# Conversions and tanh of the Scalar engine placed behind the second exponential of an even step

## What is computed

```python
q, k, v = (split_heads(x @ W.T + b) for W, b in ...)      # 16 heads of 16
scores = jnp.einsum('hbnd,hbmd->hbnm', k, q) * SCALE      # 1024 x 1024 per head, SCALE = 1/16
attn = jax.nn.softmax(scores, axis=-1)
x = layernorm(x + einsum('hbnm,hbmd->hbnd', attn, v) merged @ Wo.T + bo)
gate, up = x @ wg.T, x @ wu.T                             # hidden 768, weights int32 / 127
x = layernorm(x + (silu(gate) * up) @ wd.T)
```

## Time and profile before

| | |
|---|---|
| median of 3 runs | 2783.86 us |
| the profiled execution | 2781.8 us, its span 2779.7 us |
| TensorE busy | 2633.4 us, 95% of the span |
| Scalar engine busy | 2132.9 us, 77% |
| VectorE busy | 1291.1 us, 46% |
| GpSimd busy | 543.2 us, 20% |
| granted TensorE clock, mean | 0.994 |
| batch 0 / each batch 1 to 14 / steps of batch 15 | 149.4 / 168.1 to 168.5 / 147 us |

### The profile page before, as it was taken

One profiled execution on the slowest core, in us unless ns is written; L12 is line 12 of the kernel. 1 busy time (PEld: TensorE's weight loads), 2 busy tenths in 40 slices (PEclk: granted clock), 3 DMA queues, 4 the chain that ended last, 5 costly groups with the idle time before them and its releaser, 6 DMA issues. The chain is left out here.

```text
span 2779.7 us, 47000 instructions
## 1 busy us (share of the span) xinstructions
PE 2633.4 (95%) x17294; PEld 943.7 (34%) x17294; DVE 1291.1 (46%) x2812; ACT 2132.9 (77%) x2370; POOL 543.2 (20%) x542
## 2 busy tenths in 40 slices
PE   6889999999999999999999999999999999999996
PEld 2223332333324333342333323333243333424233
DVE  3324445454444544445444454544445444454536
ACT  2877777777787777777877787777777777787881
POOL 2101122121222112121121221112121121221113
PEclk9999999999999999999999999999999999999998
DMA  4111021210202102121120202102021020211101
GB/s 150 47 45 61 24 82 31 58 59 20 92 21 77 47 21 85 32 74 39 35 79 24 85 29 74 50 13 92 27 79 39 21 92 24 78 36 54 26 9 38
DMA packets 81742, 144.08 MB, mean 52 GB/s; under 512 B 27584, under 2 KB 29504, under 8 KB 79424
## 3 DMA queue, kind: packets, MB, share of 16 engines
q1 hardware_dynamic: 79968, 139.81, 16.4%
q10 hardware_dynamic: 1504, 0.66, 0.1%
HBM read 88.48 MB, written 50.33 MB: 50 GB/s over the span
## 5 line engine op out<-in xcount | busy, mean ns | idle before, releaser
L567 ACT ACTIVATE probs<-psum 128x1024 f32<-128x1024 f32 x2048 | 1991.3, 1026 | 548.0 <-PE psum L978 547.2
L978 PE MATMUL psum<-probs,v 128*32 128x512 f32 x8192 | 987.5, 600 | 0.8 <-ACT probs L567 0.8
L978 PE MATMUL psum<-kstack,qstack 51*128 51x512 f16 x4096 | 673.5, 383 | 87.2 <-ACT probs L567 74.8
L978 PEld LDWEIGHTS psum<-kstack,qstack 51*128 51x128 f16 x4096 | 144.9, 93 | 825.9 <-ACT probs L567 483.5
L978 PEld LDWEIGHTS psum<-probs,v 128*32 128x32 f32 x8192 | 214.1, 109 | 512.5 <-issue 510.8
L478 POOL TENSOR_TENSOR ffn<-h,ffn 128x512 f16<-128x512 f32 x192 | 222.1, 1159 | 732.7 <-DVE ffn L737 631.4
L818 DVE STREAM_TRANSPOSE flipped<-psum 128x512 f32<-128x512 f32 x128 | 91.7, 716 | 364.8 <-PE psum L978 364.8
L692 DVE SCALAR_TENSOR_TENSOR tanh_out<-tanh_out,psum 128x512 f32<-128x512 f32 x192 | 130.5, 680 | 245.4 <-ACT tanh_out L548 245.4
L457 POOL TENSOR_TENSOR squares<-parts 128x512 bf16<-128x512 f16 x128 | 134.0, 1052 | 484.7 <-DVE parts L683 484.7
L978 PE MATMUL psum<-ffn,gateT 128*128 128x512 f16 x768 | 209.4, 382 | 8.5 <-DVE tanh_out L692 8.2
L683 DVE SCALAR_TENSOR_TENSOR parts<-psum,scales,parts 128x512 f16<-128x512 f32 x128 | 94.3, 736 | 253.8 <-ACT parts L539 253.7
(11 more groups left out here) (102 smaller groups left out, 1454.9 us busy)
## 6 DMA issues: line engine op xcount, KB each, us to landing
parts_dram<-parts SPq DMA_DIRECT2D x64, 512.0 KB, 2.8
qstack<-parts_dram SPq DMA_DIRECT2D x384, 64.0 KB, 2.1
kstack<-parts_dram SPq DMA_DIRECT2D x384, 64.0 KB, 2.1
x_pre<-in_x_t SPq DMA_DIRECT2D x17, 1024.0 KB, 5.0
x_res<-in_L_attn_x SPq DMA_DIRECT2D x16, 1024.0 KB, 5.2
out<-x_res SPq DMA_DIRECT2D x32, 512.0 KB, 2.7
kstack<-shift_parts SPq DMA_DIRECT2D x384, 4.0 KB, 1.7
ffn<-in_L_ffn_w_gate SPq DMA_DIRECT2D x1, 768.0 KB, 9.4
```

The costliest lines, as they stand in the source:

```text
L567: nc.scalar.activation(probs[:, (STEPS * b + k) % SLOTS, 2 * pr:2 * pr + 2, :], scores[pr], ACT.Exp, scale=score_scale[par]).then_inc(prob ...
L978: return nc.tensor.matmul(o, lhsT, rhs, start=start, stop=stop)
```

## The change

One number in `Plan.__init__`: the conversions and tanh come half a step later in the Scalar engine's order. Nothing else is edited; TensorE's, VectorE's and GpSimd's programs and the deal of the fillers stay as they were.

```diff
             if kind in ("qk", "gate"):
-                act.append((self.ends[n] + 1.0, kind, j, n))
+                act.append((self.ends[n] + 1.5, kind, j, n))
```

## The result

The changed kernel takes **2744.4 us** (median of four runs, 2741.62 to 2744.5) against 2783.2 us before: a ratio of 0.9858 with a 95% interval of 0.984 to 0.9875. The forecast was 2743.5 us. The profiled execution has a span of 2742.3 us against 2779.7.

What follows compares the result with a forecast made beforehand. TensorE sets the time, waiting for exponentials pushed back by extra work. Gains less stalls give -2.95 us a batch, -41.3 for 14, +0.9 in batch 0: 2741.4 profiled, plus 2.1 gives 2743.5 us; range 2732 to 2758.

Steps and rivals of the forecast that it cites:

- TensorE sets the time, and a push of the second exponential is paid in full: Double steps with extra work: TensorE starts earlier by 0.39 us per conversion, 0.31 per tanh, 0.79 per two tanh.
- The extra work fits into the Scalar engine's gap: Between even and odd step's exponentials: 0.55 us gap takes a conversion (0.57) or tanh (0.48), cost taken 0.
- The cover behind it: Odd step's second exponential ends 4.76 us into the double step, not needed before 4.85: 0.09 us hides an overrun.
- The drain comes late by one exponential and TensorE waits where the freed bank is due at once: Drains 0.92 us later; double steps 22, 26, 28, 36 longer by 0.46, 0.18, 0.57, 0.12 us.
- The other twelve do not wait: Double steps 2, 4, 6, 8, 16, 18, 24, 38, 40, 42, 44, 46 keep gains of 0.39 or 0.31 us each.
- Double step 32 is held by the flip: gate3's drain stands behind the accumulator's flip on VectorE, so nothing moves: 0, the 0.79 us gain not had.
- Batches 0 and 15 give nothing: Both paced by exponentials: 0, bounds -2 to +2 us, plus 0.9 once at double step 34 of batch 0.
- Fourteen times a middle batch: Batches 1 to 14 each gain 2.95 us, 41.3 us in all.
- The first rival: More ring stalls than five, 0.85 us each; with six of the twelve stalling, 2815 us; chance 0.07.
- The second: Odd step's exponentials come late and give the gain back while the stalls stay: 2804 us; chance 0.04.
- The third: Stalls smaller than the drain chain says; without four stalls the batch gains 6.6 us: 2692 us; chance 0.06.
- the fourth: No difference: waits move from one pair of scores to the other with the same total, 2784 us; chance 0.03.

Runs made afterwards that it cites:

- the idle activation: Changed kernel plus one more 128x512 activation, writing a scratch tile, behind each conversion of the steady batches and batch 0: 2762.4 us.
- The kernel with the tanh alone: Kernel before the change with only the tanh moved behind the second exponential, conversions left between the exponentials: 2774.2 us, ratio 0.9965.
- splitting the pairs: Changed kernel with the conversion of qk6 and the tanh of gates 0, 1, 3 and 5 put back between the exponentials: 2712.6 us, ratio 0.9742.
- the last experiment: Changed kernel with all conversions and tanh one place further back, behind the odd step's first exponential (2.0 instead of 1.5): 3033 us, one run.
- the conversions alone: Kernel before the change with only the conversions moved behind the second exponential, tanh left between the exponentials: 2751.0 us, ratio 0.9884.

## Why the prediction was right

- *TensorE sets the time, and a push of the second exponential is paid in full.* Right. The pushes of 0.39 and 0.31 us came back to 0.02 us in twelve double steps. That lengths were read from start to start mattered: by the idle time of the records a conversion would have been worth 0.22 us, not 0.39.
- *The extra work fits into the Scalar engine's gap.* Right: the odd step's first exponential moved by 0.01 us. The cover behind it, which the sum did not need, is 0.24 to 0.27 us, as the idle activation showed.
- *The drain comes late by one exponential and TensorE waits where the freed bank is due at once.* Right in place and size: +0.46, +0.19, +0.60, +0.15 against +0.46, +0.18, +0.57, +0.12. The two pairs of tanh are 0.03 us off. The forecast took the gaps in VectorE's chain of four instructions over from before; in 28 the one ahead of line 733 is 0.13 us now, 0.11 before. The kernel with the tanh alone has 0.11 there, and +0.58 and +0.13. Moving conversions and tanh apart showed that each double step answers to its own extra work, to 0.02 us, and splitting the pairs took the losses away.
- *The other twelve do not wait.* Right, 18 too (-0.37 of 0.39), the one that I had called near: in batch 7 qk6's bank is free 0.13 us before it is due.
- *Double step 32 is held by the flip.* Right, and shown on the kernel before: with the flip behind the drains it falls to 5.78 us. With the pairs split as well it falls to 5.43; the changed kernel with the flip alone moved was not run.
- *Batches 0 and 15 give nothing.* Near: batch 0 has the +0.9 at double step 34 (measured +0.91), and 0.3 more at its end. Batch 15 is 0.8 us longer, at double step 10. There GpSimd's sum into `x_res` waits for its load, 9.49 us instead of 8.71, while the load is issued at the same distance from the batch's start; the data came later in this execution. The same double step is 5.53 to 6.39 us long in the nine executions traced, 5.62 and 5.64 in the two with split pairs, so it scatters also where most of the extra work is moved; a part for the change is neither shown nor excluded.
- *Fourteen times a middle batch* is the step that was a little too good, in two ways. The middle batch itself gave 2.86 us, not 2.95, by the hundredths in the table: 1.3 us in fourteen. And not every batch is a middle one. In the execution shown the first double step of batch 1 is 6.48 us long instead of 5.23: TensorE had stood for 3.00 us at the end of batch 0 and its first products took 3.29 us where 1.92 is usual. This is not the change's doing: the kernel before with only the flip moved shows 6.53 us there, the changed kernel with the idle activation 4.85. Two batches have one double step that is 0.33 and 0.37 us longer, because one VectorE instruction (line 733) starts 0.4 us late; its reason stays open.

The two spans differ by 37.4 us where 40.4 were forecast. The middle batches (1.3 us), these places (2.0), batch 15 (0.8) and the end of batch 0 (0.3) took 4.4 us, and the start of the kernel and its tail, which the sum left out, were 1.3 us shorter. So the mechanism accounts for the 40 us of the batches 1 to 14; that the median came within 0.9 us of the forecast, and not 3.0, is luck: the profiled execution before lay 2.1 us below its median, the one after at its median, and single executions of one kernel differ by 2 to 3 us.

The first rival, more ring stalls than those counted, is the mechanism of the last experiment: one place further it makes the kernel 9% slower. The second had its condition (odd exponentials late by more than their cover) in the kernel with the idle activation. The third fell with the four stalls in the table, and the fourth with the time.

## What to carry to other kernels

When work is moved along one engine's order, price two things from the timeline: who stops waiting ahead of it, and when the buffer that it frees is next due. A move helps or hurts in each place by itself, so where the trace repeats, list the places and move only those whose buffer is not due; here that turned 1.4% into 2.6%, and 3.1% with the flip. A wait that hides another (the flip ahead of gate3's drain) shows as a place that does not react.

## What the runs showed of the hardware beside that

An idle stretch of TensorE can cost more than its length, and its length alone did not tell which one does. Stalls of up to 0.88 us between busy stretches left the granted clock at 1.00 throughout batch 7 of the changed kernel. In batch 7 of the last experiment, stalls of 2.26, 2.12 and 2.11 us were followed by the lower level (windows of 0.83, 0.80 and 0.81, and four float32 matmuls that took 3.07 us instead of 1.98), while double step 28, with a stall of 2.12 us too, stayed at 1.00. The border of batches 0 and 1 shows the same. In the changed kernel 3.00 us of idle time were followed by a granted clock of 0.61, in the one with split pairs 2.16 us by 0.63; with the conversions alone TensorE stood still for 3.19 us, the clock stayed at 1.00 and the first products took 1.92 us. The changed kernel there:

```profile
203.63:208.00 4.37, 4.37 (x24) 0.82 (x24) 0.19 (x1) 1.94 (x2) 1.64 (x1) 0.61 0.40 108
```
